# One mask product for two heads: the first-pass steps that hold both heads of a pair in one bank

## The reference

```
scores = q @ k.T / sqrt(8) + slope[h] * (key - query)      # ALiBi
scores[key > query] = -inf
attn = softmax(scores) ; out = attn @ v
x = x + out @ Wo.T + bo
```

## Time and profile before

| what | value |
|---|---|
| time, median of 3 runs | 1548.06 us (1546.43 to 1549.83) |
| the profiled execution | 1548.17 us, of which its span is 1546.4 us |
| mean granted TensorE clock | 0.921 of full speed |
| PE busy | 1272.3 us (82% of the span), 12316 products |
| DVE busy | 997.0 us (64%) |
| ACT busy | 873.0 us (56%) |
| POOL busy | 379.2 us (25%) |

### The profile page before, as it was taken

The page is one execution under the profiler, slowest core; times in us unless marked ns, Lnnn a source line. Parts: engine busy times, 40 slices in busy tenths (PEclk is TensorE's granted clock), DMA queues, the critical chain, the costliest instruction groups (busy, mean ns, idle before and its releaser), DMA issues.

```text
span 1546.4 us, 35310 instructions
## 1 busy us (share of the span) xinstructions
PE 1272.3 (82%) x12316; PEld 647.1 (42%) x12316; DVE 997.0 (64%) x2120; ACT 873.0 (56%) x1107; POOL 379.2 (25%) x569
## 2 busy tenths in 40 slices
PE   3688788899888887889888897889988898976854
PEld 2333344345444443444444443444544444433323
DVE  5787666666666775666665776657666676745724
ACT  2056556666566664656655665566565666653740
POOL 4044503132031201222122110312203210424501
PEclk9589889999999998999998999999998999988986
DMA  8212414123230312313232131303313041201010
GB/s 247 65 45 86 173 38 128 31 73 116 73 117 19 117 50 65 111 33 115 80 103 66 59 107 54 112 18 114 108 58 97 20 140 36 88 30 48 18 48 15
DMA packets 108919, 120.64 MB, mean 78 GB/s; under 512 B 12097, under 2 KB 95169, under 8 KB 108737
## 3 DMA queue, kind: packets, MB, share of 16 engines
q1 hardware_dynamic: 100288, 90.38, 18.7%
q0 software_dynamic: 8448, 27.88, 6.0%
HBM read 78.63 MB, written 40.89 MB: 77 GB/s over the span
## 4 chain that ended last, share of the span: by engine, by line
PE 52%; DVE 15%; issue 14%; POOL 10%; ACT 6%; DMA 1%; POOLq 0%; DVEq 0%; ACTq 0%; SPq 0%
PE PS L1002 13%; PE PS L967 12%; DVE mx L1216 10%; PE PS L984 5%; PE PS L924 4%; PE PS L927 3%; PE PS L907 3%; PE PS L911 3%; ACT PR L797 2%; POOL xs L614 2%; POOL both L641 2%; PE PS L948 2%; PE PS L972 2%; PE PS L990 2%; PE PS L952 1%
## 5 line engine op out<-in xcount | busy, mean ns | idle before, releaser
L1216 DVE TENSOR_REDUCE mx<-PS 128x1 f32<-128x512 f32 (+3 forms) x1280 | 768.3, 633 | 351.2 <-PE PS L972 231.2
L797 ACT ACTIVATE PR<-PS 128x1024 f32<-128x1024 f32 (+3 forms) x768 | 607.4, 810 | 499.2 <-PE PS L990 311.4
L967 PE MATMUL PS<-Kop,Qop 64*128 64x512 bf16 (+3 forms) x1536 | 438.4, 346 | 140.1 <-DVE mx L1216 135.8
L984 PE MATMUL PS<-Qop,Kop 64*128 64x512 bf16 (+3 forms) x1536 | 349.0, 338 | 16.3 <-ACT PR L797 8.4
L1002 PE MATMUL PS<-PR,vbuf 128*32 128x512 f32 (+3 forms) x3072 | 342.4, 519 | 0.6 <-ACT PR L797 0.4
L967 PEld LDWEIGHTS PS<-Kop,Qop 64*128 64x128 bf16 x1536 | 130.9, 94 | 467.8 <-DVE mx L1216 371.4
L972 PE MATMUL PS<-idb,mk 64*128 64x64 bf16 x2048 | 192.0, 195 | 0.0
L972 PEld LDWEIGHTS PS<-idb,mk 64*128 64x128 bf16 x2048 | 163.4, 98 | 45.1 <-issue 7.2
L990 PE MATMUL PS<-idb,mk 64*128 64x64 bf16 x2048 | 168.3, 194 | 4.7 <-issue 4.7
L601 POOL CAST mp<-negm 128x16 bf16<-128x16 f32 x64 | 14.9, 234 | 555.2 <-DVE negm L1223 555.2
L990 PEld LDWEIGHTS PS<-idb,mk 64*128 64x128 bf16 x2048 | 136.3, 97 | 33.7 <-issue 8.3
(11 more groups left out here) (104 smaller groups left out, 1117.3 us busy)
## 6 DMA issues: line engine op xcount, KB each, us to landing
Qop<-qst SPq DMA_DIRECT2D x64, 256.0 KB, 2.8
Kop<-kst SPq DMA_DIRECT2D x64, 256.0 KB, 3.3
kst<-parts SPq DMA_DIRECT2D x32, 256.0 KB, 2.9
qst<-parts SPq DMA_DIRECT2D x16, 384.0 KB, 2.5
kst<-parts SPq DMA_DIRECT2D x32, 128.0 KB, 2.5
qst<-parts SPq DMA_DIRECT2D x16, 256.0 KB, 2.7
Qop<-mrow SPq DMA_DIRECT2D x256, 3.0 KB
onum<-osb SPq DMA_DIRECT2D x256, 16.0 KB
```

Of the source, the lines that this page charges most:

```text
L797: act.activation(PR[:, c % 4, :, 0:n], PS[:, 2 * (c % 2):2 * (c % 2) + 2, 0:n], ACT.Exp)\
L967: last = pe.matmul(PS[:, 5 + k % 2, n * e:n * e + n], Qop[r, par, a, P * i:P * i + P], Kop[r, kb, a, 512 * c:512 * c + n], start=True, sto ...
L984: last = pe.matmul(PS[:, 2 * (c % 2) + j, 0:n], Kop[r, kb, a, P * kt:P * kt + P], Qop[r, par, a, q0:q0 + n], start=True, stop=not DIAG[t])
L1216: dve.tensor_reduce(mx[:, par, i, 2 * heads[0] + j:2 * heads[-1] + j + 1:2, c], PS[:, 5 + k % 2, 0:n * len(heads)].rearrange("p (h n) -> p ...
```

## The change

In a step that has the diagonal in it, the scores of all its heads now come first. Behind them stands one mask product for each `side`, whose output is the 64 columns of that side of every head of the step (in a pair step two runs of 64 columns, `n` columns apart), and whose moving operand is the identity taken twice (a dimension of step 0). A step with one head issues the same products in the same order as before. The second head's score product doesn't set the start flag any more, since this clears the bank's marks for the first head also, whose scores now still wait for their mask.

```diff
                 for e, a in enumerate(heads):
                     last = pe.matmul(PS[:, 5 + k % 2, n * e:n * e + n], Qop[r, par, a, P * i:P * i + P],
-                                     Kop[r, kb, a, 512 * c:512 * c + n], start=True, stop=not diagonal)
-                    if diagonal:
-                        for side in range(2):
-                            at = n * e + n - P + ROWS * side
-                            last = pe.matmul(PS[:, 5 + k % 2, at:at + ROWS], mk1[r, side, :], idb[r, r],
-                                             start=False, stop=side == 1)
+                                     Kop[r, kb, a, 512 * c:512 * c + n], start=e == 0, stop=not diagonal)
+                if diagonal:
+                    heads_of_bank = PS[:, 5 + k % 2, 0:n * len(heads)].rearrange("p (h n) -> p h n", n=n)
+                    for side in range(2):
+                        at = n - P + ROWS * side
+                        last = pe.matmul(heads_of_bank[:, :, at:at + ROWS], mk1[r, side, :],
+                                         idb[r, r].unsqueeze(1).to_broadcast([ROWS, len(heads), ROWS]),
+                                         start=False, stop=side == 1)
                 last.then_inc(S["s_p1"], 1)
```

## The result

| | median | runs | range |
|---|---|---|---|
| before | 1549.86 us | 20 | 1541.4 to 1561.5 |
| after | 1542.31 us | 20 | 1526.71 to 1560.08 |

The ratio is 0.9932, with an interval of 0.9907 to 0.9958: about 10.5 us less. It leaves out the executions that lie over 1.5% above the fastest of their kernel, four of the changed kernel and none of the kernel before; with all twenty the means give 0.9950, 7.7 us. A repeat on another occasion gave 1544.27 against 1547.34 us and 0.9965 (0.9932 to 0.9998). The time lies inside the forecast range, but "the same" was forecast and the kernel is faster.

The account below looks back on a forecast made before the run. TensorE was taken as the bound (82% busy, 52% of the chain), with waits for VectorE. From 1548.17 us, 0.5 for shorter masks and 1.2 for looking ahead gave 1546.5 us, most likely the same; range 1540 to 1551.5.

Parts of the forecast that it names:

- the same: Whole kernel: a time not told from before, where about 0.2% (3.1 us) can be told; chance 0.52.
- the change part by part: 256 pair steps: shorter masks 0.5 us, earlier starts of the other half's products 1.2 us, no transfer or wait moved.
- The price of a merged mask product: Mask products of 128 columns in pair steps: 0.057 us from start to start, taken from the transposes at L879.
- the slow product: Merged masks, output in two runs and operand read twice: up to 0.125 us each, 1564.6 us in all; chance 0.09.
- The number of products: Mask line L972: 1536 products in place of 2048, 512 of them with 128 columns.
- the starts: Products within a pair step (n = 128): starts at 0, 0.06, 0.12 and 0.18 us.
- TensorE looking ahead by products: Behind pair steps: the other half's product starts right behind the step's first or second product, 0.06 to 0.15 us earlier.
- VectorE's idle time before the small pair reductions: Ahead of VectorE's reductions of 2 x 128 columns: to stay near 92 us.
- The merged steps in themselves: 256 pair steps: 0.5 us from the shorter masks and 1.2 us from earlier starts on the other half.
- looking ahead: Other half's products behind pair steps: 13.7 us of earlier starts as a bound, 1.2 us taken, from 14 places.
- The rival that looking ahead pays in full: Other half's products in 130 places: share of the chain holds, 7.1 us, 1540.6 us in all; chance 0.20.
- The clock: TensorE's 1.2 GHz stretches: one more or less, 3.4 us each, 1550 or 1543 us; chance 0.13.

Follow-up runs that it names:

- r5_pad16: The kernel before, masks untouched, with 16 semaphore increments that nobody waits for ahead of TensorE's program; 1539.89 us, ratio 0.9938 to the kernel before.
- r6_after_pad160: The changed kernel with 160 semaphore increments ahead of TensorE's program, putting the loop back to instruction 3239; 1555.93 us, ratio 1.0047 to the kernel before.
- r11_after_spread: The changed kernel with 160 increments, four behind each of the 40 opening first-pass steps; 1557.41 us, ratio 1.0027 to the kernel before.
- the unrolled pair: Changed kernel and kernel before, each with the layer loop written out on all engines; 1535.06 and 1529.21 us, ratios 0.9877 and 0.9870 to the kernel before.
- r4_late: The change for steps 16 and later only, half of the pair steps merged; 1541.13 us, ratio 0.9966 to the kernel before.
- r3_count: The changed kernel with two more one-column mask products in each pair step, as many products as before; 1570.81 us, ratio 1.0167 to the kernel before.
- r8_unrolled_before: The kernel before with the loop over layers written out on all engines; 1529.21 us, ratio 0.9870 to the kernel before.

## Why the prediction was wrong

**The step that failed** is the change part by part: it priced the steps whose products change and closed with "No transfer, no queue of SP or POOL and no wait is added or moved". The 160 instructions taken out ahead of the loop, though, move where the loop starts in the packets in which TensorE's instructions come. The term missing from the sum is the second stop, -5 us over two edges, by the stretches of after; r5_pad16 shows it without any change to the masks, and r6_after_pad160 and r11_after_spread take it back with the masks merged. It could have been seen: the chain has 14% "issue", which the prediction passed over (most of it lies elsewhere, and 13% are left in after), and the waits hold 4.7 us for two mask products of the second pass with no releaser. That there was a loop edge at both, and that an instruction count moved it, could have been a rival.

The Trainium skill (Runtime: NRT & Kernel Launch, "Instruction fetch mechanics") says that instructions come in blocks of 16 KiB, 256 to a block, that the next block is fetched while the current one runs, and that a taken branch to a target outside the current blocks forces a fetch before work goes on. The runs agree: 16.4 KB and 256 instructions in a packet, a stop of 3.0 to 4.0 us at each taken edge where it stands alone or ahead of a second one, the next packet asked for when the first one runs. The page gives no price and doesn't tell of a second stop.

**What held.** The price of a merged mask product: 0.056 us from start to start (0.057 forecast), so the slow product (rival, 0.09) is out. The number of products, the starts, TensorE looking ahead by products at the steps shown, VectorE's idle time before the small pair reductions (93.4 us before, 88.1 after). The merged steps in themselves: 1.7 us less were forecast, of which 1.2 from looking ahead. The undisturbed groups give 2.0 us, in the unrolled pair 1.8, and the times at equal clock 0.7 to 4; by itself this would have been "the same", as forecast. How much of it is looking ahead wasn't separated. With the 5.0 us of the edges the sum would have been some 7 us, where 6 were measured at equal clock. The rival that looking ahead pays in full (1540.6 us) gave nearly the measured time and is wrong as a cause: r4_late keeps half of it and loses nothing at equal clock, r5_pad16 has none of it and gains as much within 0.7 us.

**The clock.** Its rival allowed one low stretch more or less, 3.4 us. The twenty executions of before lie within 20 us and those of after within 33, these with mean clocks from 0.912 to 0.931: several stretches more or less in any execution. Between kernels the mean differed too (0.907 for r3_count, 0.929 for r8_unrolled_before); what sets it is not settled here. At the edge shown above the granted clock was 0.50, the 1.2 GHz level, from 598.3 to 605.1 before and from 593.8 to 600.6 after, each time from within or just behind the first stop on, so that an edge costs more than its stop: 5 to 7 us with one and 8 to 9 with two, by the stretches of the table beside those without an edge.

## What to carry to other kernels

An edit that changes how many instructions an engine has ahead of a loop (here TensorE) also moves the loop's start in that engine's instruction packets, and can win or lose microseconds at each back edge that have nothing to do with the edit: count the instructions, look at the "issue" rows of the first products behind an edge, and try the old kernel with a few padding instructions before crediting the edit. A gain that survives halving the edit is a sign that the edit's own work didn't make it. With three iterations, writing out the loop gave the kernel before 1.3% (0.8% at equal clock), more than the whole change; and where executions follow the clock by 9 to 15 us per 0.01, kernels are compared at equal clock or over many runs.

## What was not expected of the hardware

- At a back edge TensorE stopped for 3.0 to 4.0 us while the first instruction packet came, and 2.1 to 2.6 us more where the loop started with seven instructions of a packet left (both as one stop of 6.6 to 6.8 us with three left). With 8 or 16 padding instructions, or with 80 or 160 instructions fewer ahead of the loop, the second stop was gone; how many must be left between 7 and the 87 of r4_late wasn't tried.
- A packet of 256 instructions was usable some 2.2 to 2.8 us behind the start of its transfer, though that took 0.9 to 1.4 us.
- A mask product with its output in two runs of 64 columns and its moving operand read twice follows another in 0.056 us, like a plain one of 128 columns.
- A product on one half of the array starts ahead of products of the other half that stand before it; with two products fewer in the step it started 0.06 and 0.14 us earlier at the two steps shown, and VectorE's reductions were waited for as long as before (374.3 us, 371.4 before).
